# Batched one-hots and own edges placed with the zeros, in a graph network of two kinds of layer on one core

## The reference, cut to what matters

```python
edge_index = jnp.stack([src, dst])
# layer 0: GCN with W, batch norm over the nodes, gelu, identity added
def _gcn_conv(x, edge_index, W, b):
    xw = x @ W.T
    loop = jnp.arange(n)                       # n = N own edges, besides those given
    row = jnp.concatenate([edge_index[0], loop]); col = jnp.concatenate([edge_index[1], loop])
    deg = segment_sum(ones_like(row), col, n); dinv = where(deg > 0, rsqrt(deg), 0.0)
    msgs = (dinv[row] * dinv[col])[:, None] * xw[row]
    return segment_sum(msgs, col, n) + b
# layer 1, twice (relu between): relations r = 0, 1 with w[r] = sum_b att[r, b] * basis[b]
def rgcn_gate_layer(x, row, col, edge_type, basis, att, gate_w, root, bias):
    w = jnp.einsum('rb,bio->rio', att, basis)  # basis is 30 x 512 x 512, fp32
    ...                                        # msg = sigmoid(x_j @ gate_w[r]) * x_j @ w[r], x_j = x[col]
    return segment_sum(msg, row, n) + x @ root + bias
x = _layernorm(x + L0(x)); x = _layernorm(x + L1(x))
```

## Time and profile before

| | |
|---|---|
| median of 3 runs | 327.48 us (327.39 to 329.15) |
| the profiled execution | 326.88 us, its span 325.0 us |
| busy in the span | TensorE 283.5 us (87%), its weight loads 193.4, VectorE 175.3 (54%), ScalarE 135.3 (42%), GpSimd 36.5 |
| transfers | 73.68 MB, 227 GB/s over the span |
| mean granted clock of TensorE | 0.942 of full speed |

### The profile page before, as it was taken

One profiled execution on the slowest core, in us unless ns is written; L12 is line 12 of the kernel. 1 busy time (PEld: TensorE's weight loads), 2 busy tenths in 40 slices (PEclk: granted clock), 3 DMA queues, 4 the chain that ended last, 5 costly groups with the idle time before them and its releaser, 6 DMA issues.

```text
span 325.0 us, 4963 instructions
## 1 busy us (share of the span) xinstructions
PE 283.5 (87%) x1711; PEld 193.4 (60%) x1711; DVE 175.3 (54%) x538; ACT 135.3 (42%) x265; POOL 36.5 (11%) x71
## 2 busy tenths in 40 slices
PE   1768899885969999568999999999997999999991
PEld 1653455432336786424767656647795777787771
DVE  3878787999967847686310132233325125433333
ACT  4596868899701368647243114111313142100000
POOL 1001000000002900551000000000003600010000
PEclk9987999998695999779999999999998999999997
DMA  6974869599997999739998677975001400001112
GB/s 175 335 327 158 336 257 356 207 388 416 352 385 282 314 354 418 313 103 367 382 381 318 260 292 303 418 294 246 2 0 32 132 0 0 2 0 33 33 34 63
DMA packets 12759, 73.68 MB, mean 227 GB/s; under 512 B 1952, under 2 KB 2195, under 8 KB 4540
## 3 DMA queue, kind: packets, MB, share of 16 engines
q1 hardware_dynamic: 11282, 70.82, 57.4%
q0 software_dynamic: 1104, 2.36, 2.8%
q10 hardware_dynamic: 346, 0.17, 0.3%
HBM read 72.05 MB, written 1.28 MB: 226 GB/s over the span
## 4 chain that ended last, share of the span: by engine, by line
PE 61%; DVE 22%; issue 7%; DMA 4%; DVEq 2%; ACT 1%; POOL 1%; ACTq 0%; POOLq 0%
PE psW L495 13%; PE psM L476 10%; PE psM L477 9%; PE psM L478 9%; PE psM L717 6%; PE psM L737 6%; DVE oh_key L1047 4%; DMA basis_ring<-in_L_gnn_basis_dram 3%; PE psM L623 3%; DVE B L1038 2%; PE psE L570 2%; DVEq L1032 2%; DVE w L1027 1%; DVE x_sum L1170 1%; DVE AT L1103 1%
## 5 line engine op out<-in xcount | busy, mean ns | idle before, releaser
L495 PE MATMUL psW<-basis_ring,S 128*32 128x512 f32 x512 | 68.2, 651 | 3.2 <-DMA basis_ring<-in_L_gnn_basis_dram 3.1
L1217 DVE SCALAR_TENSOR_TENSOR zg<-psM,gate,zg 125x512 fp32r<-125x512 f32 x20 | 15.0, 751 | 59.5 <-ACT zg L891 59.5
L1047 DVE TENSOR_SCALAR oh_key<-iota_f,key 128x160 f16<-128x160 f16 x162 | 36.0, 262 | 2.6 <-PE psE L570 1.4
L785 ACT ACTIVATE oh_diff<-iota_f,edgeT 128x128 f16<-128x128 f16 x108 | 34.1, 389 | 3.4 <-DVEq L964 3.4
L495 PEld LDWEIGHTS psW<-basis_ring,S 128*32 128x32 f32 x512 | 13.9, 115 | 32.5 <-issue 26.4
L476 PE MATMUL psM<-w,hlT 128*125 128x512 f32 x80 | 33.1, 414 | 0.1
L891 ACT ACTIVATE zg<-psM,gate 125x512 fp32r<-125x512 f32 x20 | 13.8, 688 | 46.1 <-PE psM L478 45.7
L477 PE MATMUL psM<-w,hlT 128*125 128x512 f32 x80 | 32.3, 404 | 0.0
L478 PE MATMUL psM<-w,hlT 128*125 128x512 f32 x80 | 32.1, 402 | 0.0
L570 PEld LDWEIGHTS psE<-oh_key,oh_src 128*125 128x125 f16 x162 | 16.0, 150 | 25.2 <-issue 19.2
L570 PE MATMUL psE<-oh_key,oh_src 128*125 128x160 f16 x162 | 21.3, 261 | 10.2 <-issue 6.6
(11 more groups left out here) (159 smaller groups left out, 430.5 us busy)
## 6 DMA issues: line engine op xcount, KB each, us to landing
basis_ring<-in_L_gnn_basis_dram SPq DMA_DIRECT2D x64, 1024.0 KB, 7.1
root_raw<-in_L_gnn_root_dram POOLq DMA_DIRECT2D x32, 64.0 KB, 3.6
xs<-in_x_dram SPq DMA_DIRECT2D x1, 1120.0 KB
out_dram<-xs SPq DMA_DIRECT2D x5, 224.0 KB
w_raw<-in_L_gnn_W_dram SPq DMA_DIRECT2D x1, 1024.0 KB, 10.9
bias_b<-in_L_gnn_bias_dram POOLq DMA_DIRECT2D x1, 250.0 KB, 3.8
xs<-in_x_dram SPq DMA_DIRECT2D x1, 130.0 KB
out_dram<-xs SPq DMA_DIRECT2D x5, 26.0 KB
```

What stands on the lines that cost most here:

```text
L495: m = nc.tensor.matmul(psW[32 * j:32 * j + 32, cc % 2, :], S[:, cc % 2, cc // CH, q].rearrange("p k r -> p (k r)"), ring[:, n % RING, j, : ...
L785: nc.scalar.activation(oh_diff[:, g % 3, j * P:(j + 1) * P], iota_f[:, 0:P], ACT.Abs, bias=edgeT[:, 0, g * G + j:g * G + j + 1], scale=-1. ...
L1047: v.tensor_scalar(oh_key[:, t % OH, :], iota_f[:, 0:KEYS], key[:, t:t + 1], None, ALU.is_equal) \
```

## The change

VectorE makes both one-hots of a whole group in one comparison each. iota and the numbers to compare with are read in pairs of 16-bit values, for which places and keys are stored twice side by side. `oh_key` gets room for three groups, ScalarE makes no one-hots, and the two column look-ups of a group stand ahead of its comparisons.

```diff
-            for t in range(T):
-                    dve.wait_ge(adj_used, t - OH + 1)
...
-                v.tensor_scalar(oh_key[:, t % OH, :], iota_f[:, 0:KEYS], key[:, t:t + 1], None, ALU.is_equal) \
+            def one_hots(out, pairs, first, n, width):
+
+                pair = iota_f[:, 0:width].rearrange("p (k i) -> p k i", i=2)
+                shape = [P, n, width // 2, 2]
+                return v.tensor_tensor(out, pair.unsqueeze(1).broadcast_to(shape),
+                                       pairs[:, first:first + n].unsqueeze(2).broadcast_to(shape), ALU.is_equal)
+
+            for g in range(NG):
+                if g >= 3:
+                    dve.wait_ge(adj_used, G * (g - 2))
+                at = [window_at(w) for w in range(2 * (g - 2), 2 * (g - 1))] if g >= 2 else []
+                src = oh_src[:, g % 3].rearrange("p (t e) -> p t e", t=G)[:, :, 0:PLACES]
+                one_hots(src.rearrange("p t (k i) -> p t k i", i=2), place_pairs, g * G, G, PLACES)
+                one_hots(oh_key[:, g * G % OH:g * G % OH + G].rearrange("p t (k i) -> p t k i", i=2), key_pairs, g * G, G, KEYS) \
                     .then_inc(key_ready, 1)
...
+                    dve.wait_ge(b_zero, NC)
+                for i in TURNED_LOW_AT.get(g, ()):
+                    turned_low(i)
+                for i, w in enumerate(range(2 * (g - 2), 2 * (g - 1)) if g >= 2 else ()):
+                    add_window(w, at[i])
+                if g == ROUNDS_AT:
                     rounds()
+                if g in MERGE_AT:
+                    w_merge(MERGE_AT[g])
+                if g in LOW_AT:
+                    w_low(LOW_AT[g])
             for w in range(NW - 4, NW):
-                add_window(w)
+                add_window(w, window_at(w))
...
+            v.tensor_copy(place_pairs[:], edgeT[:, 0, :].unsqueeze(2).broadcast_to([P, T, 2]))
...
+            link(v.tensor_copy(key_pairs[:], key[:].unsqueeze(2).broadcast_to([P, T, 2])))
```

```diff
-            act.wait_ge(place_ready, 1)
-            for g in range(NG):
-                places(g)
...
             for c in range(NC):
-                link(v.tensor_tensor(AT[:, c], B[:, c, 0, 0:N2], B[:, c, 1, 0:N2], ALU.add))
-                d = AT[:, c, c * PC:(c + 1) * PC]
-                v.tensor_tensor(d, d.bitcast(F32), ident[0:PC, 0:PC], ALU.add).then_inc(at_ready, 1)
-            w_merge(2)
+                v.tensor_tensor(AT[:, c], B[:, c, 0, 0:N2], B[:, c, 1, 0:N2], ALU.add).then_inc(at_ready, 1)
...
             for c in range(NC):
-                last = v.tensor_scalar(diag[:, c, :], ident[0:PC, 0:PC], dinv_p[:, c:c + 1], None, ALU.mult)
-            last.then_inc(diag_ready, 1)
...
-            for h, (c0, c1) in enumerate(((0, 4), (4, NC))):
-                wait_full(dve, ("dinv", h))
-                link(v.tensor_copy(dinv_b[:, c0 * PC:c1 * PC], bank(("dinv", h))[:, 0:(c1 - c0) * PC]))
-                dve.sem_inc(free_dve, 1)
-
+            w_merge(1)
+            dve.wait_ge(dinv_b_ready, 2)
...
+            for d in range(NC):
+                own_edge = BB[:, d * (R * NC + 1) * PC:(d * (R * NC + 1) + 1) * PC]
+                last = v.tensor_tensor(own_edge, own_edge.bitcast(F32), ident[0:PC, 0:PC], ALU.subtract)
+            link(last)
...
 in GpSimd's list:
-                    last[0] = nc.tensor.transpose(bank("vec")[:, at:at + NV], rows[:, k * P:(k + 1) * P], ident[0:NV, 0:NV])
+            for k in range(KC):
+                last[0] = nc.tensor.transpose(bank("vec")[:, k * NV:(k + 1) * NV], vec_rows_q[:, k * P:(k + 1) * P],
+                                              ident[0:NV, 0:NV])
             done()
-            basis_upto(24)
             wait_free(pe, "deg")
...
 in TensorE's list, behind agg0 (0, 0):
+                    if (f, h) == (0, 0):
+                        pe.wait_ge(diag_ready, NC)
...
 in ScalarE's list, behind z:
+            for i, (c0, c1) in enumerate(((0, 4), (4, NC))):
+                wait_full(act, ("dinv", i))
+                link(nc.scalar.activation(dinv_b[:, c0 * PC:c1 * PC], bank(("dinv", i))[:, 0:(c1 - c0) * PC], ACT.Copy))
+                act.sem_inc(free_act, 1)
+                act.sem_inc(dinv_b_ready, 1)
```

```diff
+            for j in range(JB):
+                sp.dma_start(w0_raw[32 * j:32 * j + 32], W0.rearrange("(k c j) o -> j k c o", k=2 * KB, c=KC)[j]) \
+                    .then_inc(w0_in, 16)
...
-                                            in1=natural(bank(("g", c))[0:PC, :]), op0=ALU.mult, op1=ALU.add))
+                                            in1=in_q(bank(("g", c))[0:PC, :]), op0=ALU.mult, op1=ALU.add))
```

```diff
-                if FIRST_XW <= g < FIRST_XW + NC * KC // 2:
...
-                basis_upto(9 * g // 10)
+                if FIRST_XW <= g < FIRST_XW + NC * KC:
+                    xw_part(g - FIRST_XW)
+                basis_upto(min(2 * g // 3 - 2, PARTS_IN))
...
-                basis_upto((28, 30, 31, 32)[f])
-            basis_upto(33)
+                basis_upto((21, 23, 25, 27)[f])
...
+            basis_upto(29)
...
-                basis_upto((35, 36, 37)[c])
+                basis_upto((31, 33, 35)[c])
...
-                    basis_upto(39 + KC * h + f)
+                    basis_upto((37, 37, 39, 39, 41, 41, 43, 43)[KC * h + f])
...
-                            basis_upto(47 + 7 * (R * c + r) // 5)
+                            basis_upto((45, 47, 47, 49, 51, 51, 53, 55, 55, 57)[R * c + r])
...
-                    basis_upto(min(60 + KC * h + f, 2 * CH * SUB - 1))
+                    basis_upto((57, 59, 59, 61, 61, 63, 63, 63)[KC * h + f])
```

More of the change, by code:

```diff
@@ L255, in gnn_block @@
         use("deg", "dve")
-        for h in range(2):
-            use(("dinv", h), "dve")
         NBB = -(-NC * R * NC // 4)
@@ L264, in gnn_block @@
                 use(("agg0", f, h), "dve")
+                if (f, h) == (0, 0):
+                    for i in range(2):
+                        use(("dinv", i), "act")
                 for b in BB_STEPS[2 * f + h]:
@@ L430, in _ @@
             nc.gpsimd.tensor_tensor(dinv_p[:], deg[:], mhalf[0:PC, 0:NC], ALU.pow).then_inc(dinv_ready, 1)
+            pool.wait_ge(dinv_ready, 1)
+            for c in range(NC):
+                nc.gpsimd.tensor_scalar(diag[:, c, :], ident[0:PC, 0:PC], dinv_p[:, c:c + 1], None, ALU.mult) \
+                    .then_inc(diag_ready, 1)
             pool.wait_ge(at_ready, NC)
@@ L604, in _ @@
             done()
[L605 to L614 removed]
+            basis_upto(17)
+            basis_upto(19)
             for f in range(KC):
@@ L626, in _ @@
                     done()
+                    if (f, h) == (0, 0):
+                        pe.wait_ge(diag_ready, NC)
+                        for i, (c0, c1) in enumerate(((0, 4), (4, NC))):
+                            wait_free(pe, ("dinv", i))
+                            for c in range(c0, c1):
+                                last[0] = nc.tensor.matmul(bank(("dinv", i))[:, (c - c0) * PC:(c - c0 + 1) * PC],
+                                                           ones_f[0:PC, :], diag[:, c, :], start=True, stop=True)
+                            done()
                     for b in BB_STEPS[2 * f + h]:
```

143 lines of the change are left out of this document (54 added, 89 removed).

## The result

The changed kernel takes **350.84 us** (median of 4 runs, 348.58 to 352.98), the kernel before, beside it, 327.44 (326.60 to 329.15): ratio 1.071, 95% interval 1.063 to 1.079. I had said 339, in a range of 320 to 357. The direction holds; the loss is 23.4 us and not 11.5.

| | before | after | change | by the sum on record |
|---|---|---|---|---|
| last addition into B | 93.97 | 106.36 | +12.4 | +10.4 |
| from there to the copy of deg | 8.86 | 7.04 | -1.8 | -2.55 |
| to the end of the second aggregate product | 8.0 | 9.7 | +1.7 | +2.5 |
| to the transposes of hf (`g`) | 22.1 | 27.8 | +5.7 | +0.3 |
| to the first root product | 16.7 | 20.4 | +3.7 | -2.6 |

A forecast was written before the change was run, and what follows sets the result against it. VectorE was taken to bound the edge-group loop, TensorE nearly everything from 150 us on. Loop +10.4, degrees -2.55, then +2.5, +0.3, -2.6, +1.4 and +1.9 make +11.4; with 326.88 and 0.6 that is 339 us, range 320 to 357.

The forecast's parts named there:

- The comparisons, two elements a cycle: VectorE's two batched 16-bit comparisons per group run at two elements a cycle: 0.55 and 0.66 us.
- The look-ups of the next group begin when the second addition is handed over: Edge-group loop: VectorE's queue cannot run ahead, two look-ups show (about 1.05 us); a group takes 2.78 us, before 1.83.
- The loop, +10.4: Loop over 27 edge groups: 89.8 us for 80.1, last addition into B from 94.0 to 104.3, +10.4 us.
- Degrees, -2.55: First AT to copy of deg: 5.1 us instead of 7.64, without own edges and the merge before the copy.
- In front of the aggregates, +2.5: Four basis parts instead of two start the first aggregate 1.3 us late; spreading behind it adds 1.3: +2.5 us.
- Aggregates to gelu, +0.3: ScalarE's first half for the fourth weight pair stands ahead of the last gelu: +0.3 us net.
- x1, -2.6: x1 and root: a 2.43 us merge leaves the chain, x_sum reads one strided operand less; TensorE's extra parts fill idle time.
- The wait for w_merged and the two parts more, +3.3: Pair behind the first root product waits for the late merge, +1.4 us; 28 parts left instead of 26, +1.9.
- ten parts must land in 30 us: Transfers from the aggregates' end to the first root pair fit at 2.7 us a part; up to 2 us waits uncounted.
- Hidden look-ups: Rival: queue runs ahead in the loop, a group takes 1.75 us; 316 us, partly hidden 320 to 326; chance 0.18.
- one element a cycle: Rival: batched comparisons run at half the assumed rate, 0.86 us more a group, 23 in all: 362 us; chance 0.10.
- The third: Rival: TensorE's clock falls in the loop and TensorE sets the pace, 7 to 14 us more: 346 to 353; chance 0.09.

The follow-up runs named there:

- the table of ratios: Loop of before or changed loop, each with weight places of before or changed, against the kernel before: 1.003 and 1.024, 1.045 and 1.071.
- c1: Changed kernel with the loop of before and the weight work at its places of before; 328.09 us, 1.003 to the kernel before.
- e1: Changed kernel, its own loop kept, with the weight work at its places of before (24 parts in the loop); 342.72 us, 1.045 to the kernel before.
- a1: Changed kernel with a group's two column look-ups behind its comparisons instead of ahead of them; 332.49 us, 1.014 to the kernel before.
- d1: Changed kernel with look-ups behind the comparisons and the weight work at its places of before; 324.86 us, 0.995 to the kernel before.
- h1: d1 with the diagonals on VectorE and their spreading ahead of the first aggregate, as before; 324.22 us, 0.990 to the kernel before.

## Why the prediction was wrong in size, step by step

- *The comparisons, two elements a cycle*: right, 0.65 and 0.55 us (0.66 and 0.55 forecast).
- *"The look-ups of the next group begin when the second addition is handed over"*, 2.78 us a group: right, 2.77 to 2.80, and shown by the moved line to be what the loop loses.
- *The loop, +10.4*: too small by 2.0 at the last addition (12.4). The steady groups are right. What I had too cheap is what stands between them: the three with two low parts behind the comparisons take 4.73, 5.12 and 4.81 us, some 0.7 us more together than the forecast has for them; the start of the loop, up to the third group (14.47 to 22.04), takes some 0.5 us more; and twice VectorE's queue itself stood still for 0.4 us between a load and its register operation (ahead of 52.09 and 81.41), for which I know no cause. By the table of ratios the loop is worth 13.8 to 15.2 us, by the spans of the same traces 12.5 and 13.5.
- *Degrees, -2.55*: -1.8 in the trace. The own edges do what was said; the first AT comes 1.6 us behind the last addition instead of 1.2, and the copy of deg 5.45 us behind it instead of 5.1. The diagonals on GpSimd, which I had at 0.4 us each, take 0.59 to 0.86.
- *In front of the aggregates, +2.5*: +1.7 measured in the changed kernel. But part of it is the spreading behind the first aggregate, which costs with the weight work at its old places too; c1 ends up at 1.003 in spite of its earlier deg.
- *Aggregates to gelu, +0.3*: +5.7. Of it 2.5 are waits for transfers (1.97 and 0.51), 1.6 the lower clock behind the first of them (2.60, 1.06 and 2.00 us for operations that take 1.73, 0.62 and 1.65), and 1.4 ScalarE's `w_high(2)` and `w_first(3)` in front of the last gelu, which I had priced at 0.3.
- *x1, -2.6*: +3.7. 3.9 us of waits for transfers, and the gain was 0.5 even without them: "eight parts instead of four, in time that was idle" was wrong, as the half transfers show. `x_sum` stays at 1.02 us, so the one operand less in the other order was worth nothing.
- *The wait for w_merged and the two parts more, +3.3*: +1.2 by the table, but that is partly luck. In the trace of before TensorE's clock falls once more in this stage, behind a wait of 1.67 us in the second layer: from 249.92 to 253.44 its products start 0.42 to 0.53 us apart, at full clock 0.23 to 0.34. That is 1.6 us; only the traces of before and c1 have it, the twelve others do not. Against e1, whose stage takes 173.9 us, the changed kernel's is 2.7 longer.
- **The step that failed** is the sentence "From the aggregates' end to the first root pair ten parts must land in 30 us; it fits, with up to 2 us of waits that I leave out of the sum." I had looked at one window of the transfers only. The account must begin where the schedules part: eight parts (8 MB) fewer are used in the loop, and by the windows some 6 MB less are moved in it (205 GB/s over 92.4 us, before 316 over 80). The four parts in a row then empty the ring, and what follows needs 20 parts where before it was 14, at 2.7 us each where transfers are near their limit and at 3.3 us beside root1. Measured in the changed kernel: 2.5 us of waits among the aggregates, which that account does not reach at all, 1.6 us of lower clock behind them, and 3.9 us of waits in x1 where it allows "up to 2"; in time 7.5 us by the half transfers, 6.9 to 8.3 by the table.
- *The rivals.* Hidden look-ups and one element a cycle are excluded. The third had the right time (346 to 353) for a wrong reason: TensorE's granted clock over the loop did fall, to 0.80 from 0.91, but it did not set the pace; steady groups take 2.77 to 2.80 us at 0.50 and at 0.99 alike, and 1.98 with the look-ups moved. The Trainium skill ("TensorE: Matmul & The Clock Gate", Part 1) has the low level as the default that activity lifts, and the trace agrees that the clock falls where TensorE idles more (0.50 from 26 to 44 us). The time near 350 that the prediction drew from it hit the number and not the cause.

## What to carry to other kernels

An instruction of the queue (a column from memory into a register) is free only while the engine still has queued work: put it behind the longest operation, not at the head of a group. When loads feed a small ring, a schedule is judged by how much is used by the end of each stage, since a full ring stops the transfers: work moved out of an idle stage comes back as transfer time in a busy one. And an operation moved off a waiting engine's path must be followed to where it now stands: the spreading, the halves of root1 and the pairs in x1 each became the next limit.

## What the runs showed of the hardware

- A comparison of two 16-bit tensors, both read in adjacent pairs and broadcast over the rest: 0.546 us for 756 elements (median in a1, d1 and h1; 0.553 in the changed kernel) and 0.652 for 960, by which an element takes 0.52 ns, with 0.15 us fixed.
- While GpSimd makes the five diagonals (0.59 to 0.85 us each, 3.60 together in c1, where VectorE needs 1.06), VectorE's z beside it takes up to 0.85 us a chunk, 3.73 for five; before it took 3.40, and in h1, with the diagonals on VectorE again, 3.39 (0.75 a chunk). Why was not tried.
- TensorE's clock can fall or stay behind the same wait: behind the 1.67 us of the second layer it fell in the traces of before and c1 and stayed at its full level in the twelve others.
